# Graph attention over 8192 nodes: ten blocks of each tile turned in five transposing DMAs of two blocks, their products one slot later

## The reference

```python
h = jnp.maximum(_layernorm(x, axis=-1), 0.0)
scores = jnp.einsum('nd,md->nm', h, ks)
scores = jax.nn.leaky_relu(scores, negative_slope=0.2)
scores = jnp.where(adj > 0, scores, -9e15)
attn = jax.nn.softmax(scores, axis=1)
out = x + jnp.einsum('nm,md->nd', attn, ks)
```

## Time and profile before

| | us |
|---|---|
| median of 3 runs (1595.24 to 1597.04) | 1596.42 |
| the profiled execution, its own time | 1591.91 |
| its span in the profile | 1590.0 |

### The profile page before, as it was taken

How to read it: one execution, slowest core, us unless ns; L and a number is a source line. 1 busy time by engine, 2 the same in 40 slices (tenths; PEclk the granted TensorE clock), 3 DMA queues, 4 the chain that set the end, 5 groups by cost and what they waited for, 6 DMA issues and landing times.

```text
span 1590.0 us, 37555 instructions
## 1 busy us (share of the span) xinstructions
PE 1560.3 (98%) x13202; PEld 1156.2 (73%) x13202; DVE 1418.5 (89%) x2527; ACT 1342.3 (84%) x2008; POOL 1329.5 (84%) x1348
## 2 busy tenths in 40 slices
PE   5899999999999999999999999999999999999998
PEld 3577777777777777777777777777777777777777
DVE  7998998999899899889889989998998998999896
ACT  6788888888888888888888888888888888888886
POOL 3688888888888888888888888888888888888885
PEclk9999999999999999999999999999999999999999
DMA  9999999999999999999999999999999999999995
GB/s 315 282 276 274 293 282 279 277 284 277 280 283 274 283 280 263 275 281 279 275 267 298 273 280 279 292 270 271 295 263 289 268 279 285 282 282 281 269 282 94
DMA packets 701626, 437.67 MB, mean 275 GB/s; under 512 B 629760, under 2 KB 629760, under 8 KB 701440
## 3 DMA queue, kind: packets, MB, share of 16 engines
q1 hardware_dynamic: 701440, 435.27, 112.7%
HBM read 276.82 MB, written 4.19 MB: 177 GB/s over the span
## 4 chain that ended last, share of the span: by engine, by line
PE 94%; DMA 1%; POOL 1%; DVE 1%; ACT 1%; issue 0%; POOLq 0%; DVEq 0%; ACTq 0%
PE ps_out L434 27%; PE ps_out L435 14%; PE ps_scores L408 13%; PE ps_scores L409 13%; PE ps_scores L407 13%; PE ps_T L418 12%; DMA keys_in<-keys_in 1%; PE ps_out L433 0%; PE ps_out L384 0%; ACT scores L505 0%; POOL keys_in L348 0%; POOL keys_in L346 0%; DVE scores L628 0%; PE ps_out L432 0%; ACT scores L496 0%
## 5 line engine op out<-in xcount | busy, mean ns | idle before, releaser
L348 POOL TENSOR_TENSOR keys_in<-scores,keys_in 128x512 f16<-128x512 f32 x572 | 720.6, 1260 | 46.1
L628 DVE CUSTOM_DVE_ANT_0 scores<-ps_scores,mask,minus_scale 128x1024 f32<-128x1024 f32 x512 | 653.9, 1277 | 16.1 <-PE ps_scores L409 1.2
L496 ACT ACTIVATE scores<-scores 128x1024 f32<-128x1024 f32 x512 | 538.0, 1051 | 77.9 <-DVE pair_min L628 77.9
L346 POOL CAST keys_in<-scores 128x512 f16<-128x512 f32 x572 | 460.0, 804 | 162.6 <-ACT scores L505 159.5
L505 ACT ACTIVATE scores<-scores,neg_max 128x1024 f32<-128x1024 f32 x512 | 583.4, 1140 | 0.1
L434 PE MATMUL ps_out<-keys,keys_in 128*128 128x256 f16 x2225 | 428.6, 273 | 3.1 <-DMA keys_in<-keys_in 3.1
L643 DVE TENSOR_TENSOR probsT_lo<-ps_T,probsT_hi 128x512 f16<-128x512 f32 x452 | 310.6, 687 | 123.6 <-ACT probsT_hi L513 114.9
L407 PE MATMUL ps_scores<-keysT_hi,hT_hi 128*128 128x512 f16 x1024 | 389.0, 380 | 13.9 <-DVE keysT_lo L599 9.7
L435 PE MATMUL ps_out<-keys,keys_in 128*128 128x128 f16 x2225 | 398.0, 219 | 0.0
L513 ACT ACTIVATE probsT_hi<-ps_T 128x512 f16<-128x512 f32 x447 | 264.5, 592 | 155.5 <-PE ps_T L418 152.1
L408 PE MATMUL ps_scores<-keysT_lo,hT_hi 128*128 128x512 f16 x1024 | 389.0, 380 | 0.0
(11 more groups left out here) (57 smaller groups left out, 825.7 us busy)
## 6 DMA issues: line engine op xcount, KB each, us to landing
adj_in<-in_adj_dram SPq DMA_DIRECT2D x512, 512.0 KB, 5.3
keys_in<-keys_in SPq DMA_TRANSPOSE x572, 5.6
x_in<-in_x_dram SPq DMA_DIRECT2D x16, 256.0 KB, 4.0
keys_in<-in_L_gnn_ks_dram SPq DMA_DIRECT2D x8, 512.0 KB, 7.1
out_dram<-out_tile SPq DMA_DIRECT2D x16, 256.0 KB, 4.1
keys<-keysT_hi SPq DMA_TRANSPOSE x8, 4.7
keys<-keysT_lo SPq DMA_TRANSPOSE x8, 4.6
```

The source lines that it names most:

```text
L346: nc.gpsimd.tensor_copy(half[:, 0:BLOCK], probs(t, b)).then_inc(half_hi_ready, 1)
L348: nc.gpsimd.tensor_tensor(half[:, BLOCK:2 * BLOCK], probs(t, b), half[:, 0:BLOCK], ALU.subtract) \
L496: nc.scalar.activation(s, s, ACT.Prelu, alpha=1.0 / SLOPE).then_inc(leaky_ready, 1)
L628: nc.vector.tensor_tensor_reduce(out=score_pair(q, p), in0=ps_scores[:, slots, :].rearrange("p s k -> p (s k)"), in1=mask[:, (p // 2) % 2, ...
```

## The change

The set of blocks that go by DMA gains block 4, and in the last tile block 8, so it has ten (six). SyncE issues one transposing DMA for two consecutive blocks of the ring, when the second of them is split: (1, 3), (4, 5), (7, 9), (11, 12), (13, 15). The ring of turned blocks has ten slots and one semaphore for each two. The products of turned blocks stand one slot later (ADD_LAG 11), and finish (VectorE), the transpose of the normalised rows (TensorE) and its split (VectorE) move one slot later too.

```diff
-    D_SLOTS = 8
+    D_SLOTS = 10
-    ADD_LAG = 10
-
-    BY_DMA = tuple(b for b in range(BLOCKS) if b % 2 == 1 or b in (12,))
+    ADD_LAG = 11
+
+    BY_DMA = tuple(b for b in range(BLOCKS) if b % 2 == 1 or b in (4, 12))
-    LAST_BY_DMA = (1, 3, 5, 7, 9)
-    LAST_BY_DVE = (0, 2, 4, 6, 8)
+    LAST_BY_DMA = (1, 3, 5, 7, 8, 9)
+    LAST_BY_DVE = (0, 2, 4, 6)
...
-        turned_in = [sem(f"turned_in{s}") for s in range(D_SLOTS)]
+        turned_in = [sem(f"turned_in{s}") for s in range(D_SLOTS // 2)]
...
-            def turn(t, b):
+            def turn_two(t, b):
+
                 n = nth_dma(t, b)
                 sp.wait_ge(half_lo_ready, n + 1)
...
-                sp.dma_start(turned[:, n % D_SLOTS, :, :], halves[:, n % R_SLOTS, :], transpose=True) \
-                    .then_inc(turned_in[n % D_SLOTS], 16)
+                to, of = (n - 1) % D_SLOTS, (n - 1) % R_SLOTS
+                sp.dma_start(turned[:, to:to + 2, :, :].rearrange("p s k c -> p (s k) c"),
+                             halves[:, of:of + 2, :].rearrange("p s k -> p (s k)"), transpose=True) \
+                    .then_inc(turned_in[to // 2], 16)
...
-                        if turning:
-                            turn(*turning)
+                        if turning and nth_dma(*turning) % 2 == 1:
+                            turn_two(*turning)
...
-                    pool.wait_ge(turned_in[m % D_SLOTS], 16 * (m // D_SLOTS + 1))
+                    pool.wait_ge(turned_in[m % D_SLOTS // 2], 16 * (m // D_SLOTS + 1))
...
-                pe.wait_ge(turned_in[n % D_SLOTS], 16 * (n // D_SLOTS + 1))
+                pe.wait_ge(turned_in[n % D_SLOTS // 2], 16 * (n // D_SLOTS + 1))
...
-                    if j == 12 and ahead:
+                    if j == 13 and ahead:
                         transpose_h(i + 2, odd)
...
-                    if ahead and j == 13:
+                    if ahead and j == 14:
                         split_h(i + 2, odd)
...
-                    if prev and j == 10:
+                    if prev and j == 11:
                         finish(i - 1, 1 - odd)
```

## The result

The kernel after takes 1733.16 us (median of 4, 1730.03 to 1742.9) against 1596.06 us before: ratio 1.0869, 95% interval 1.0824 to 1.0914. That is 137 us slower. I had forecast 1577.5 us, and my range ended at 1600.

What follows compares the result with a forecast made beforehand. TensorE was taken to bound the kernel at 24.09 us a tile. TensorE and GpSimd at about 23.66 plus 0.12 gave 23.78, saving 19.2 us over 62 tiles, less 1.5: net 17.7; forecast 1577.5 us, range 1567 to 1600.

Steps and rivals of the forecast that it cites:

- What bounds the kernel now: TensorE's own work sets the pace, 24.09 us a tile; GpSimd is next, occupied 21.82 us.
- The step that failed: SyncE and its DMA queue: room of 7.0 us a tile, and 315 GB/s shown where 287 is needed.
- Removed from TensorE: Block 4's four transposes leave TensorE: 0.44 us a tile less, so 23.65 us alone.
- imperfect fit: Allowance of 0.12 us a tile for uneven turns with TensorE and GpSimd both near 23.66, giving 23.78 us.
- the joint bound: GpSimd's one more split adds 1.84 us, so its occupation becomes 23.66 us a tile, level with TensorE.
- Rival C: GpSimd loses more than 1.84 us; one more mask stall of 0.86 us makes its tile 24.5 us; chance 0.10.
- by the trace nothing: VectorE's masks lose nothing to a busier GpSimd; by the skill page up to 1.16 us a mask.
- d: Time from the end of a split to its turned block's landing: 7.2 us before, 8.5 us for a pair.
- Rival B: Two-block DMAs make the turn's time take over: d over 9.6 us means slower, 1622 us at d = 10; chance 0.13.
- The later slots: Finish, x_norm transpose and its split one slot later, on engines with free time: nothing, at most 5 us.
- What would show it: Signs in the profile after: fewer transposes, more splits, x_norm interval near 23.8 us, GpSimd's waits for ScalarE near 0.
- Issue to landing at 9 or above: Sign in the DMA rows that d was wrong; about 7 us was expected.

Runs made afterwards that it cites:

- e13: Kernel before, with one 128x128 transpose in place of four on TensorE for blocks 4 and 8 from the second tile on: 1594.3 us, ratio 0.9961.
- e1: Kernel after with its pairing undone: ten transposing DMAs of one block each a tile, later slots kept: 1718.1 us, ratio 1.0735.
- e6: Kernel before plus one transposing DMA a tile that no compute engine waits for: 1707.6 us, ratio 1.0670.
- e10: Kernel after with ten one-block DMAs a tile, and products and other steps in the slots of before: 1709.2 us, ratio 1.0674.
- e11: Kernel before plus two transposing DMAs a tile that no compute engine waits for: 1795.2 us, ratio 1.1211.
- e12: e1 (ten one-block DMAs, later slots) with every adj load from the second tile on fetching half its columns: 1566.8 us, ratio 0.9786.
- e16: Kernel after whole, pairs and later slots, with adj loads of half their columns: 1599.4 us, ratio 0.9988.
- e5: e1 without block 4's DMA except in the first and last tile; all ten splits stay, nine DMAs run: 1602.5 us, ratio 1.0015.
- e4: Kernel before with 30 lone transposing DMAs of 256 to 2048 columns behind its last store, on an empty queue or behind a load; issues up to 3.53 us.
- e2: Kernel after with nine blocks a tile as before, still in two-block DMAs (4.5 a tile) and later slots: 1671.7 us, ratio 1.0447.
- e9: Kernel before with only the slots moved: nine one-block DMAs, ten turned slots, products and other steps one slot later: 1666.7 us, ratio 1.0412.
- e15: Kernel before with nine one-block DMAs, ten turned slots and only the products one slot later: 1594.6 us, ratio 0.9963.
- e8: e7 with its four 1 MB loads issued by ScalarE on its own queue: 2378 to 2485 us.
- e7: e1 with adj in four loads of 1 MB a tile in place of eight of 0.5 MB: 1806.2 us, ratio 1.1286.

## Why the prediction was wrong

*What bounds the kernel now.* "The pace is TensorE's own work" was right as far as it went, and not enough. I looked for the next engine among the compute engines and found GpSimd. The next bound was the DMA queue, and it was not next but nearly level: e13.

*The step that failed.* "SyncE waits for GpSimd's splits 407.5 us in the stretch, 7.0 us a tile, so it has room", and "the first slice of the page shows 315, so the queue can carry it". The first misreads the list of waits: SyncE's pauses do not add up to anything like 407.5 us, so the list counts time in which it was still issuing. SyncE's timeline before the change, with no pause worth the name:

```profile
803.96 3.67 SPq L269 DMA_TRANSPOSE keys_in<-keys_in  x1
807.69 0.57 SPq L258 DMA_DIRECT2D adj_in<-in_adj_dram  x1
808.35 1.44 SPq L269 DMA_TRANSPOSE keys_in<-keys_in  x1
```

In the steady stretch its issues add up to 1294 of 1400 us, and its pauses of more than 0.3 us to 34: 0.6 us a tile of room, not 7.0. Those pauses shrink to 4 or 5 us in e1, e6, e10, e11 and e13, and grow to 248 in e12 and 310 in e16. I had priced a turn's issue by its least, 1.23 us; its mean was 1.91. The second reads the wrong slice: the first holds mainly the start's loads. The steady slices ran at 263 to 298 GB/s, mixed of loads and turns, 279 over the stretch, and every kernel with more turns and full loads moved less: 253 to 268. The price of one more turn is 1.7 us a tile (e6), not the 0.8 us of its bytes. This term, which I priced at nothing in the tile's length, is 6.7% (e10) of the 8.7% lost.

*Removed from TensorE, 0.44 us a tile:* the size was right. In e12 a tile lasts from the x_norm transpose at 798.43 to the next at 822.14, 23.71 us; I had 23.66 for both engines and 23.78 with imperfect fit. That is 24 us of the 33 by which e12 beats before; the other 9 lie outside the steady tiles, and the kernel before with half loads was not run to tell them apart.

*GpSimd's tenth split, the joint bound at 23.66 us:* right, where the queue has room (e12: both full, TensorE without a gap). Rival C, more stall on GpSimd, was not the cause: casts and subtractions average 751 and 1247 ns in the kernel after, 804 and 1260 before.

*The masks.* I took "by the trace nothing" for VectorE's loss, and set the trace's x_norm row against the Trainium skill's "SBUF — State Buffer" (on who interferes with whom; the page says it of VectorE instructions in a two-port mode or with two inputs from SBUF, a condition that I left out). With a GpSimd that rests less the page was right: a mask that begins inside a subtraction is stretched by most of what is left of it (e5: 0.80 us in the row shown, with 0.94 left), and masks average 1.53 us in the kernel after, 1.71 in e5. This is the second term that failed: with room in the queue TensorE waits in e16 for VectorE alone, 25.0 us, and e16 takes 1599.4 us where e12 takes 1566.8. The x_norm row stays as it is, unexplained by the page; one row was too little to set aside the rule.

*The pairing and d.* I priced the pair's issue at up to 2 x 1.23 us; it takes 3.4 and more behind a load (e4). I had d = 8.5 us; in the example shown it is 6.2 us of SyncE's lateness plus 5.3 to the landing, 11.5, and by the averages 3.7 + 6.5, about 10.2. Rival B named this mechanism ("the turn's time takes over"), with a price for d = 10 of 25 us and 0.13 as its chance. But it put the cause in the pair. With the queue full the pair's own share is small: 1.3% over e1, and e2's 0.3% over e9 is within the noise. With room it is open: e16 takes 2% more than e12, but with the long masks that e5 has without pairs. The Trainium skill's "DMA: Bandwidth & Descriptors", in its comparison of issue times, by which I took it that an issue would grow with its size, is not borne out by e4: 1.23 us at 1024 columns and 1.28 to 1.44 at 1536, then a jump that depends on what is ahead.

*The later slots, priced at nothing, at most 5 us:* with nine blocks they cost 67 us (e9). With ten they cost little, 1.0735 against 1.0674 with the queue full, intervals that overlap, and with room e12 shows no wait from them. So this term was not what failed here, but by luck: I had not asked where the moved steps would push the masks.

*What would show it.* "If TensorE waits for the turned tile tens of microseconds with GpSimd idle too, B" is what the profile shows. Transposes and splits changed as I said, but the x_norm interval averages 26.4 us in the steady stretch, not 23.8. "Issue to landing at 9 or above" was the wrong measure: it reads 6.5, since the lateness lies ahead of the issue.

A version that beats both kernels is e15, 1594.6 us: by 0.4%, interval 0.2 to 0.55%. It is a small thing, and says that with nine blocks only the products should move.

## What to carry to other kernels

A busy engine with no waits proves only that nothing else is longer, not that nothing else is as long; before trading its work for DMAs, ask what the DMA queue does in the same stretch, and price a DMA by what one more of them costs in the steady mix, not by the best slice. Read the room of the engine that issues the DMAs from its own timeline, as the pauses between its issues, and not from the list of waits. Two cheap probes answer this in one run each: a DMA that no compute engine waits for, and the bound engine's work made lighter. An engine given more work also changes when its neighbours' instructions meet it; check the mean length of theirs. When a change moves several steps "one slot later", move them one at a time.

## What the runs showed of the hardware

- In this mix of loads from HBM and transposing DMAs on one queue, one more transposing DMA of 0.262 MB costs 1.7 us, a second 1.4 us (e6, e11).
- A transposing DMA's issue on SyncE takes 1.17 to 1.24 us up to 1024 columns and 1.28 to 1.44 at 1536; at 2048 it takes 1.3 to 1.9 on an empty queue, 3.4 to 3.5 behind a load of 0.5 MB (e4).
- With the turns on SyncE's queue and the loads of 1 MB on ScalarE's, the kernel took 2378 to 2485 us against 1806 with both on one (e8, e7).
- VectorE's mask instruction is stretched by a GpSimd subtraction already under way, 1.22 to 2.02 us (e5), as GpSimd's are by the mask. All 110 long masks of e9's steady stretch and all 174 of e5's began inside a subtraction, with 0.8 us of it left on average, and were 0.7 us longer than 1.22.
